# A language-model tower on one core: more products without a reader ahead of waits, the last expert tiles written out, and one GpSimd instruction fewer per add

## The reference

```
h = token_embedding(x, itok, ...)                 # word, position, gated word vector, layer norm
h = h + L0_attn(layernorm(h), ...)                # linear attention with running sums, 12 heads of 16
h = h + L0_ffn(layernorm(h), ...)                 # routed: 19 of 128 tokens attend, the others are mixed; then 192->768->192
h = h + L1_attn(layernorm(h), ...)                # softmax attention, low-rank projections, biases
h = h + L1_ffn(layernorm(h), ...)                 # 8 experts, each token to its top 2, 192->768->192
```

```
hidden = gelu(x @ w1[e] + b1[e]);  out += weight * (hidden @ w2[e])
```

## Time and profile before

| | |
|---|---|
| three runs, median (lowest to highest) | 850.01 us (849.41 to 850.13) |
| the profiled execution | 846.64 us, of which the span is 844.8 us |
| PE busy | 734.1 us, 87% of the span |
| DVE, ACT, POOL busy | 505.8, 300.7, 232.8 us |
| mean granted clock | 0.968 |
| chain that ended last, by engine | PE 55%, DVE 23%, issue 6%, POOL 4%, DMA 4%, ACT 4% |
| front(0), then joint passes | about 42 to 149, 149 to 292, 292 to 436, 436 to 571 us |
| back, and expert tiles | from 571 us; PE's first transposes of a tile at 641 us, its last product at 831 us |
| the last add starts | 834.67 us |

### The profile page before, as it was taken

The page is one execution under the profiler, slowest core; times in us unless marked ns, Lnnn a source line. Parts: engine busy times, 40 slices in busy tenths (PEclk is TensorE's granted clock), DMA queues, the critical chain, the costliest instruction groups (busy, mean ns, idle before and its releaser), DMA issues.

```text
span 844.8 us, 15945 instructions
## 1 busy us (share of the span) xinstructions
PE 734.1 (87%) x5710; PEld 542.6 (64%) x5711; DVE 505.8 (60%) x1707; ACT 300.7 (36%) x698; POOL 232.8 (28%) x281
## 2 busy tenths in 40 slices
PE   1798777989889998988998898899989999999992
PEld 0545455466657646655764665675856989999992
DVE  6558668773769787367977546884345543333330
ACT  0024132433443262434416244333333433333330
POOL 5242110452001346100322200132001454443442
PEclk9899999999999999999999999989999999999997
DMA  7960000000000100000010000016601233222220
GB/s 252 415 282 1 1 1 1 19 8 1 2 2 3 56 19 8 1 3 1 20 39 1 1 1 2 2 38 255 213 2 30 44 76 49 38 43 35 42 32 9
DMA packets 29621, 43.22 MB, mean 51 GB/s; under 512 B 5146, under 2 KB 24451, under 8 KB 29556
## 3 DMA queue, kind: packets, MB, share of 16 engines
q1 hardware_dynamic: 19264, 30.98, 10.4%
q0 software_dynamic: 8432, 8.53, 5.8%
q10 hardware_dynamic: 1860, 2.84, 0.9%
HBM read 20.92 MB, written 22.09 MB: 51 GB/s over the span
## 4 chain that ended last, share of the span: by engine, by line
PE 55%; DVE 23%; issue 6%; POOL 4%; DMA 4%; ACT 4%; SPq 1%; DVEq 0%; POOLq 0%; ACTq 0%
PE qa L1930 25%; PE qc L1930 24%; PE qc L1933 4%; PE qa L1933 3%; DMA out<-qk_T 3%; DVE mx L1506 2%; DVE st L1070 2%; DMA mu_row<-in_mu 1%; ACT big L824 1%; DVE arena_e L1318 1%; POOL arena_w L444 1%; DVE qk_T L1512 1%; ACT wT L791 1%; POOL rs_a L479 1%; DVE ctxT L1461 1%
## 5 line engine op out<-in xcount | busy, mean ns | idle before, releaser
L1930 PE MATMUL qc<-arena_w,big 128*128 x468 | 83.0, 327 | 2.1 <-DVE qk_T L1909 1.4
L1930 PEld LDWEIGHTS qc<-arena_w,big 128*128 128x128 f32 x468 | 75.1, 190 | 3.3 <-issue 3.2
L1930 PE MATMUL qa<-arena_e,nT 128*128 128x192 f32 (+2 forms) x256 | 69.3, 426 | 2.3 <-DVE ga L1388 2.0
L1930 PE MATMUL qa<-arena_b 128*128 128x128 f32 (+2 forms) x688 | 69.9, 281 | 1.0 <-ACT arena_b L781 0.8
L621 POOL DMA_INDIRECT out<-qk_T x39 | 63.7, 1633 | 19.6 <-POOL spare L620 9.9
L1036 ACT ACTIVATE big<-qa,arena_b 128x128 f32<-128x128 f32 x156 | 43.0, 375 | 72.2 <-PE qc L1930 67.3
L1930 PEld LDWEIGHTS qa<-arena_b 128*128 128x128 f32 (+2 forms) x688 | 64.0, 187 | 6.4 <-ACT arena_b L781 1.4
L1930 PEld LDWEIGHTS qa<-arena_e,nT 128*128 128x128 f32 x256 | 45.9, 195 | 24.8 <-issue 14.6
L1909 DVE TENSOR_SCALAR qk_T<-qc,qk_T 128x192 f32<-128x192 f32 x39 | 16.3, 417 | 65.3 <-PE qc L1930 60.4
L479 POOL TENSOR_TENSOR rs_a<-rs_a,minus_half 128x8 f32<-128x8 f32 x4 | 6.6, 1642 | 170.8 <-DVE rs_a L1355 170.8
L1933 PE MATMUL qa<-cst,arena_b 128*128 128x128 f32 (+2 forms) x232 | 33.7, 286 | 9.5 <-DVE arena_e L1318 4.0
(11 more groups left out here) (393 smaller groups left out, 1555.7 us busy)
## 6 DMA issues: line engine op xcount, KB each, us to landing
slots<-xk SPq DMA_DIRECT2D x1, 13192.0 KB, 41.3
arena_e<-in_w SPq DMA_DIRECT2D x8, 579.0 KB, 7.6
arena_w<-in_w SPq DMA_DIRECT2D x8, 576.0 KB, 8.5
qk_T<-slots SPq DMA_DIRECT2D x39, 97.0 KB, 2.0
out<-hb SPq DMA_DIRECT2D x16, 96.0 KB, 1.7
arena_e<-in_w_l SPq DMA_DIRECT2D x1, 816.0 KB, 8.1
arena_e<-in_W ACTq DMA_DIRECT2D x1, 768.0 KB
out<-qk_T POOLq DMA_INDIRECT x39, 3.6
```

Of the source, the lines that this page charges most:

```text
L1930: return nc.tensor.matmul(o, l, r, start=start, stop=stop)
```

## The change

There are four parts.

1. In the front, the `stream` call ahead of `qk_turn` goes from 4 to 6 products and the one ahead of `scores` from 2 to 5. Seven `hold` calls are new: 5 ahead of `on_T`, 1 ahead of `select`, 2 ahead of `queries`, 1 ahead of `words_T`, 4 and 2 ahead of the two `mix`, 2 ahead of `selected`. That is 5 products of 512 columns and 17 of 256.
2. In each joint pass, at a first place 2 ahead of `kq`, 1 ahead of each `x5_T` and 1 ahead of the next `qk_turn`; at a second place 2 ahead of `select`. Together 7 of 256 columns per pass, 21 in all.
3. Tiles 12 to 38 are written out on SP, TensorE, DVE, ACT and POOL, with constants where registers were. For the last tile the gelu's six instructions each raise `m_gelu`, and `down` waits ahead of each of its six products for one of them.
4. The instruction with the waits ahead of each add goes, with its semaphore; the indirect DMA takes the waits on `m_y` and `m_add` itself. The same instruction ahead of the scatters and gathers (L496) stays.

```diff
         def tiles(engine, do):
-            with engine.Fori(0, (MT - EARLY) // RING) as r:
-                for u in range(RING):
-                    do(r * RING + (u + EARLY), u, r + EARLY // RING)
-            for u in range(MT % RING):
-                do(MT // RING * RING + u, u, MT // RING)
+            for tile in range(EARLY, MT):
+                do(tile, tile % RING, tile // RING)
...
-            with sp.Fori(0, (MT - EARLY) // RING) as r:
-                for u in range(RING):
-                    sp.wait_ge(m_add, r * (16 * RING) + 16 * (EARLY - RING + u + 1))
-                    slot_load(r * RING + (u + EARLY), u)
-            for u in range(MT % RING):
-                sp.wait_ge(m_add, 16 * (MT // RING * RING - RING + u + 1))
-                slot_load(MT // RING * RING + u, u)
+            for tile in range(EARLY, MT):
+                sp.wait_ge(m_add, 16 * (tile - RING + 1))
+                slot_load(tile, tile % RING)
...
             def add(tile, u, turn):
                 pool.wait_ge(m_y, tile + 1)
-                since(pool, carried, tile)
                 since(pool, m_add, tile * 16)
-                pool.tensor_tensor(spare[:, 0:1], minus_half[:, 0:1], minus_half[:, 0:1], ALU.add).then_inc(carried, 1)
                 pool.indirect_dma_start(
...
             def gelu(tile, u, turn):
...
+                last = isinstance(tile, int) and tile == MT - 1
                 for j in range(FJ):
                     i = A(hTm[:, u % 2, j, :], PS[u % 2][:, j % 2, j // 2 * 128:j // 2 * 128 + 128], ACT.Gelu,
                           bias=w1s[u % 3][:, F + FJ // 2 * 128 + j:F + FJ // 2 * 128 + j + 1])
-                i.then_inc(m_gelu, 1)
+                    if last or j == FJ - 1:
+                        i.then_inc(m_gelu, 1)
...
                 for j in range(FJ):
+                    if last and j:
+                        pe.wait_ge(m_gelu, tile + 1 + j)
```

The products, front first (one line of context around each), then the two places of the joint pass:

```diff
-                stream(4)
+                stream(6)
                 qk_turn(ta, 0, 0, True)
...
+                hold(QC[:, 0, :], 5)
                 on_T(ta, 0)
...
-                stream(2)
+                stream(5)
                 scores(ta)
...
+                hold(QC[:, 0, :], 1)
                 select(ta)
+                hold(QC[:, 0, :], 2)
                 queries(ta)
                 select_T(ta)
+                hold(QC[:, 0, :], 1)
                 words_T(ta + 1)
...
+                hold(QC[:, 0, :], 4)
                 mix(ta, 0)
+                hold(QC[:, 0, :], 2)
                 mix(ta, 1)
...
+                hold(QC[:, 0, :], 2)
                 selected(ta, 0)
...
+                hold(QC[:, 3, :], 2)
                 kq(ta, 0)
+                hold(QC[:, 3, :], 1)
                 x5_T(tb, 0)
+                hold(QC[:, 3, :], 1)
                 x5_T(tb, 1)
+                hold(QC[:, 0, :], 1)
                 qk_turn(ta, 1, 0)
...
+                hold(QC[:, 3, :], 2)
                 select(ta)
```

More of the change, by code:

```diff
@@ L89, in build @@
             sem(n) for n in ("fills", "setup_v", "setup_p", "setup_a", "slots_empty"))
-        route, scattered, carried = (
-            sem(n) for n in ("route", "scattered", "carried"))
+        route, scattered = (
+            sem(n) for n in ("route", "scattered"))
         slot_in = [sem(f"slot_in{u}") for u in range(RING)]
```

## The result

The changed kernel takes 841.73 us (median of 4 runs, 840.91 to 843.63), the kernel before 849.71 us beside it. The medians are 8.0 us apart, where 9.8 were forecast. The ratio is 0.9915, interval 0.9896 to 0.9935, which is a gain of 7.2 us with bounds of 5.5 and 8.8. The profiled execution took 841.68 us. That is close to the changed kernel's median, while the profiled execution of the kernel before (846.64 us) was 3.1 us faster than that kernel's median, so the two profiles are only 5.0 us apart. Lines of the changed kernel stand 7 to 9 lower than before: products are L1923, transposes L1926, the add's DMA L612. L1420 of before, the DVE instruction that needs the queries, is L1413 now. L1413 of before, an earlier DVE instruction that needs `select` through ScalarE, is L1406 now.

What follows compares the result with a forecast made beforehand. Mostly TensorE bounds the kernel, with nine stretches at 1.2 GHz totalling 37.5 us. Clock gains of 9.65 us plus 1.8 for adds make 11.5, less 1.7 gives 9.8: 850.0 to 840.2 us, range 836 to 846.

Steps and rivals of the forecast that it cites:

- The front, 4.35 us: Front: three low-clock stretches at full clock give 4.8 us, less 0.45 for the one product ahead of `select`.
- at full clock 1.7 us less: Front, 95.20 to 98.70 us: the stretch filled with the output projection, on the chain, gets 1.7 us shorter at full clock.
- First place, 4.7 us: First place of the joint passes: full-clock projections and transposes gain 2.1, 1.7 and 1.4 us, less 0.5 for products sticking out.
- the cost there is 0 if the clock stays up: Second place, joint passes: two products push `select` back 0.9 us, cancelled at full clock; about 0.9 per pass otherwise.
- Pass three, 0.6 us: Second place of pass three: DVE's 0.63 us wait for the route logits goes at full clock.
- The first rival: Second place keeps its clock drops: 3 × 0.9 us paid, 0.6 not won, 843.5 us; chance 0.15.
- The adds, 1.8 us: POOL's chain of adds in the expert tiles: 0.5 us saved per add, 1.5 for the last three plus 0.3 early.
- starts 0.29 us after what it waits for: Cost of an indirect DMA that waits by itself, read once at the program's start; basis for 0.5 us saved per add.
- Loop 0, last gelu 0, tiles 4.53 us: Expert tiles: writing out the loop and splitting the last gelu gain nothing; a tile stays at 4.53 us.
- One stretch of full worth left or new: Whole kernel: one low-clock stretch remains or appears elsewhere, taking 1.7 us off the 11.5 us gain.
- the signs that it named: Front 4 us earlier, joint passes 1.4 to 2.5 each, add's DMA 0.3 us after landing, 1.9 us projections, 4.53 us tiles.
- The fourth rival, slower: POOL's adds: own DMA waits cost 1.5 us, landing plus start passes 4.53 us (from 0.95), 860 us; chance 0.05.

## Why the prediction was right, and where it was off

Direction and mechanism hold on the first chip: the clock's gains and little else. The products alone give 4.9 us; the loop, the add's instruction and the last gelu each give nothing that a time shows (the loop alone 0.9999; L620 put back 0.9919 beside 0.9915; the gelu whole 0.9992 beside 0.9985). From these parts one would add up some 5 us, and in the profiles the span fell by 4.9, while the ratio says 7.2 and the medians 8.0. The 2.3 us between 0.9942 and 0.9915 lie within the two intervals; that the parts help one another is not shown.

That 841.73 us came so near to the 840.2 of the forecast is in part luck. The prediction also said that the profiled execution would go from 846.64 to about 836.8 us, and it went to 841.68: term by term, the profiles account for 4.9 of the 9.8 us. The rest of the medians' 8.0 us is that the profiled execution of the kernel before was 3.1 us faster than its median; what the slower executions lose, no trace shows. The terms, as far as the profiles show them:

- **The front, 4.35 us.** Measured 3.5: 1.3 at `on_T` (term 1.7), 1.0 at the broadcast (1.7), 1.2 around the route logits, with `select`'s cost in it (1.4 − 0.45). The term that was mis-sized is "at full clock 1.7 us less" for a low stretch that is filled; why 0.4 and 0.7 us of it don't reach DVE was not looked into.
- **First place, 4.7 us.** Measured 2.1 + 1.7 + 0.8 = 4.6. The terms were 1.8, 1.6 and 1.3.
- **Second place, "the cost there is 0 if the clock stays up".** This step failed. The clock stayed up in passes one and two, and each lost 0.6 us. The queries were in time. The prediction asked only whether L1420 would wait for the queries. L1413 of before, L1406 now, needs `select` through ScalarE and comes earlier on DVE; it now waits 0.63 us. Taking one of the two products away left a loss of 0.13 in pass one, and taking both a gain of 0.17.
- **Pass three, 0.6 us.** The first rival held here in the profiled execution (low for 10.2 us, +2.7), and the forecast in two other kernels on that chip with the same products (−0.6). The same products keep the clock in one execution and not in the next.
- **The adds, 1.8 us.** This step failed too: that an indirect DMA which waits by itself "starts 0.29 us after what it waits for". That row waits for POOL's own instruction just before it. A DMA that waits for a landing itself starts 0.72 us after the last step of its sequencer; with L620 ahead it is 0.18 us of work and 0.52 of issue, nearly the same. The tail gave 0.4 us against the profile of before and 0.27 against that with L620 put back, both within the scatter of the tail, where 1.5 was forecast; the interval between the last two adds gave 0.05 to 0.06.
- **Loop 0, last gelu 0, tiles 4.53 us:** all as forecast. The prediction sets the loop's even pace against a stall on a branch whose target isn't loaded. No load of instructions starts between 737.3 and 827.0 us of the kernel before, so the loop's code was there and did not meet that case; its pace neither bears out such a stall nor speaks against it.
- **"One stretch of full worth left or new", 1.7 us:** of this size. Low stretches of 1.7 us each appeared in single profiles at 143.6, 312.8, 314.3 and 456.3.

Of the signs that it named, no low stretch around 95, 112 and 126 us, projections of 1.9 us and 4.53 us a tile came. The front ended 3.5 us earlier instead of 4, passes one and two gained 1.5 and 1.1 us and pass three lost 1.9, where 1.4 to 2.5 each was forecast, and the add's DMA starts 0.83 us after the landing instead of 0.3.

The fourth rival, slower, is excluded by the row: landing to DMA is 0.83 us, under its 0.95, and a tile takes 4.53 us. What no rival had was the other chip, where the gain is gone.

The best version by these runs has no product ahead of `select`: 0.9904 on the first chip, where it can't be told from the change, and 0.9918 on the third, where the change stands at 0.9985.

## What to carry to other kernels

Products that keep TensorE's clock up are free only where TensorE waits anyway. Ahead of a short step on the path they cost up to their own length through the first reader on any engine (here 0.75 of 1.05 us), so look for the earliest reader and not the largest. The cost of a wait is read from a row that waits for the same kind of thing, a landing for a landing. A pair of profiles is compared only after looking at where each stands among its kernel's times. And a gain that rests on the clock has to be timed on more than one chip: here it was 0.85% on one, and 0.15% on another, which can't be told from none.

## What the runs showed of the hardware

- The clock can fall while TensorE is never idle: at 545.6 us of the changed kernel it was busy 4.12 of the 4.12 us ahead of the fall (541.50 to 545.62) and all through the stretch behind it, and 3.40 of 3.40 ahead of a fall of before. Gate products of 8 columns and selections of 20 run there. The kernel with the products alone was as busy there (4.00 of 4.00 us, 541 to 545) and kept the full clock, so what decides is open.
- Executions of the same code differ by whole low stretches: of the four profiles on the third chip, whose programs are the same up to 250 us, two show one at 144 us (1.7 us) and two don't.
- On two of three chips, at one step of each joint pass, TensorE's result reached ScalarE 2.1 to 5.5 us after the start of its transposes instead of 0.65, and always 2.46 to 2.87 us behind the start of the scatter's last DMA. In the changed kernel's trace on the third chip the low clock followed each time, behind the fourth scatter too (3.4 to 10.2 us), and the four losses are some 24 us in all. Nothing of it shows in the 4.53 us of the later tiles, which are the same on all three chips.
- An indirect DMA that waits for a landing itself starts 0.72 us after the last step of its sequencer (825.50 to 826.22), 0.83 us after the landing; back to back in the scatter it is 0.30 (`[0.30 <-issue]` ahead of each L534).
